# Layer 0 start-up of a fused attention and expert kernel: the first two batch rows are projected first, the other keys are projected dense and spread by transfers

## The reference

```python
x = x + xattn0(layernorm(x), ctx)     # 16 heads of 8; softmax(q k^T / sqrt(8)) v, out projection
x = x + ffn0(layernorm(x))            # 8 experts, each token goes to the one with the largest logit; relu^2
x = x + xattn1(layernorm(x), ctx)     # the same shape, scores clipped, other weights and biases
x = x + ffn1(layernorm(x))            # 8 experts, the best two by softmax(logits / 5), gelu
```

## Time and profile before

| | |
|---|---|
| median of 3 runs | 242.5 us (242.43 to 242.52) |
| profiled execution, first to last instruction | 242.5 us, so nothing of its time lies outside its span |
| PE busy | 225.4 us, 93% of the span |
| DVE, ACT, POOL busy | 164.2, 121.9, 79.8 us |
| mean granted clock of TensorE | 0.993 of full |
| start to first maxima of layer 0 | 16.84 us |

### The profile page before, as it was taken

How to read it: one execution, slowest core, us unless ns; L and a number is a source line. 1 busy time by engine, 2 the same in 40 slices (tenths; PEclk the granted TensorE clock), 3 DMA queues, 4 the chain that set the end, 5 groups by cost and what they waited for, 6 DMA issues and landing times.

```text
span 242.5 us, 6733 instructions
## 1 busy us (share of the span) xinstructions
PE 225.4 (93%) x2534; PEld 173.1 (71%) x2534; DVE 164.2 (68%) x513; ACT 121.9 (50%) x231; POOL 79.8 (33%) x105
## 2 busy tenths in 40 slices
PE   7999989999998999999987799998999999999993
PEld 7347668776666999998874556777656777766773
DVE  2697668656654865569438675797328974799994
ACT  2653456564674566655600377565435356443340
POOL 8592400001061177745450794564510100000000
PEclk9999999999999999999999999999979999999999
DMA  7990422314014013421122110213000000001001
GB/s 209 392 395 12 118 56 53 90 49 137 3 44 123 0 56 87 135 80 34 44 55 58 45 49 26 69 49 110 27 0 4 0 0 0 3 0 46 3 0 43
DMA packets 12451, 16.38 MB, mean 68 GB/s; under 512 B 1428, under 2 KB 9620, under 8 KB 12292
## 3 DMA queue, kind: packets, MB, share of 16 engines
q1 hardware_dynamic: 10068, 12.87, 17.2%
q0 software_dynamic: 1152, 2.24, 3.2%
q10 hardware_dynamic: 1200, 0.85, 1.1%
HBM read 11.31 MB, written 3.95 MB: 63 GB/s over the span
## 4 chain that ended last, share of the span: by engine, by line
PE 68%; DVE 17%; DMA 7%; issue 3%; POOL 2%; ACT 1%; DVEq 0%; ACTq 0%; SPq 0%; POOLq 0%
PE ps L1240 12%; PE ps L1252 12%; PE ps L1063 10%; PE ps L1108 6%; PE ps L1320 5%; PE ps L1330 5%; DVE mx L681 5%; PE ps L1071 4%; DVE xn L663 4%; PE ps L973 4%; DMA moe_y<-ys,tok_i 3%; DMA work<-moe_y 2%; DVE stats L649 2%; POOL rstd L367 2%; DMA xr<-in_x 2%
## 5 line engine op out<-in xcount | busy, mean ns | idle before, releaser
L681 DVE TENSOR_REDUCE mx<-ps 128x4 f32<-128x512 f32 x64 | 41.0, 685 | 15.6 <-PE ps L1063 15.6
L517 ACT ACTIVATE PT<-ps 128x512 f32<-128x512 f32 x64 | 35.7, 590 | 27.7 <-PE ps L1071 27.7
L1063 PE MATMUL ps<-k,q 32*128 32x128 f32 x512 | 36.1, 282 | 6.8 <-DVE mx L681 5.7
L1063 PEld LDWEIGHTS ps<-k,q 32*128 32x128 f32 x512 | 30.8, 186 | 16.2 <-DVE mx L681 12.9
L1071 PE MATMUL ps<-q,k 32*128 32x128 f32 x512 | 37.2, 283 | 0.0
L1252 PEld LDWEIGHTS ps<-proj,work 128*128 128x128 f32 x256 | 30.7, 192 | 5.7 <-issue 5.7
L627 ACT ACTIVATE work<-ps,fc 128x512 f32<-128x512 f32 x32 | 21.5, 687 | 24.4 <-PE ps L1240 22.9
L1071 PEld LDWEIGHTS ps<-q,k 32*128 32x128 f32 x512 | 31.1, 186 | 1.9 <-issue 1.7
L1240 PE MATMUL ps<-xT,fc 128*128 128x512 f32 x64 | 31.5, 617 | 0.0
L1252 PE MATMUL ps<-proj,work 128*128 128x128 f32 x256 | 31.1, 275 | 0.0
L403 POOL DMA_INDIRECT moe_y<-ys,tok_i x22 | 21.8, 991 | 24.1 <-DVE ys L899 12.0
(11 more groups left out here) (156 smaller groups left out, 314.4 us busy)
## 6 DMA issues: line engine op xcount, KB each, us to landing
proj<-in_proj SPq DMA_DIRECT2D x1, 2048.0 KB, 12.2
fc<-in_fc SPq DMA_DIRECT2D x8, 256.0 KB, 3.3
slots_x<-xs SPq DMA_DIRECT2D x2, 709.5 KB, 12.4
fc<-in_w SPq DMA_DIRECT2D x8, 129.0 KB, 2.3
proj<-in_w SPq DMA_DIRECT2D x8, 128.0 KB, 2.5
wr<-in_wr SPq DMA_DIRECT2D x1, 913.0 KB, 7.9
xs<-slots_x SPq DMA_DIRECT2D x2, 322.5 KB, 3.8
xs<-slots_x SPq DMA_DIRECT2D x2, 258.0 KB, 3.0
```

Source lines behind the costliest of these rows:

```text
L517: nc.scalar.activation(PT[:, j % PTR, :], ps[:, ring_at(layer, ("st", j)), :], ACT.Exp, scale=SCALE).then_inc(b_done, 1)
L681: nc.vector.tensor_reduce(mx[:, b, 4 * g:4 * g + 4], ps[:, S_BANK(layer, j), :].rearrange("p (k m) -> p k m", m=M), axis=AX, op=ALU.max).t ...
L1063: ins = mm(ps[:, S_BANK(layer, 2 * n + i), P * k:P * k + P], q4[r:r + 32, k, L * b:L * b + L], k4[r:r + 32, k, M * b:M * b + M], start=Tru ...
```

## The change

- Rows 0 and 1 are taken alone at first: statistics, `rsqrt`, normalisation (`first_normalise`), transposes, and queries and keys in products of 256 columns (`first_keys`, `queries(0, i)`). `ln_stats(0, 1)` then covers rows 2 to 7, whose normalisation stands in DVE steps 0, 1 and 2, two rows each.
- Keys of rows 2 and 3 (256 columns, step 0) and of rows 4 to 7 (512 columns, step 1) are each one dense product, spread by four SP transfers each (`keys_in`). Before them POOL writes the constants of `k4` (`k_fill`, two instructions that read zeros of `q4`, which ACT now clears).
- Queries of rows 2 and 3 follow in steps 2 and 3. The transposes of rows 4 to 7 and the values of rows 4 to 7 stand in step 4, the dense queries of rows 4 to 7 in step 5, the values of rows 0 to 3 in step 6. The idle products of layer 0 are gone.
- POOL clears `vaug` only after the last normalisation; `second_key_bias` stands in DVE step 3, `v_evac(1)` in step 4, `v_evac(0)` in step 6, `context_sums` in tile 5 of the expert layer.
- `proj` is loaded in eight pieces beside `fc`, the empty slots are written after rows 2 and 3, and `wa` is 128 + 1 columns wider (the dense key weights).

```diff
@@ SP
-            sp.dma_start(proj[:], proj_in).then_inc(s_fc, 16)
+            def keys_in(part, lo, hi):
+                for g in range(4):
+                    sp.dma_start(k4[32 * g:32 * g + DH, :, lo:hi],
+                                 k_dense[32 * g:32 * g + 32, lo - 256:hi - 256]).then_inc(k_in[part], 16)
@@ shift_rows
+                    if layer == 0 and b == 0:
+                        sp.wait_ge(k_sb, 6)
+                        keys_in(1, 512, 1024)
...
                         sp.dma_start(fc[:, b, :], fc_in[:, b, :]).then_inc(s_fc, 16)
+                        sp.dma_start(proj[:, b], proj_in[:, b]).then_inc(s_fc, 16)
+                    if layer == 0 and b in (2, 3):
+                        empty_slots(b - 2)
...
+            sp.wait_ge(k_fill, 1)
+            sp.wait_ge(k_sb, 5)
+            keys_in(0, 256, 512)
             shift_rows(0)
@@ POOL
             rsqrt(0, 0)
+            pool.wait_ge(first_norm, 1)
+            pool.wait_ge(dve_const, 1)
+            pool.wait_ge(q_fill, 1)
+            nc.gpsimd.tensor_scalar(k4[:, :, 256:512], q4[:, :, 512:768], shift_row[:, 0:1], None, ALU.subtract)
+            nc.gpsimd.tensor_scalar(k4[:, :, 512:1024], q4[:, :, 512:1024], shift_row[:, 0:1], None, ALU.subtract).then_inc(k_fill, 1)
             rsqrt(0, 1)
+            pool.wait_ge(ln_norm, 2)
             nc.gpsimd.memset(vaug[:], 0.0).then_inc(v_clear, 1)
...
-            nc.gpsimd.memset(q4[:, :, 512:1024], 0.0).then_inc(q_fill, 1)
+            pool.wait_ge(k_fill, 1)
+            pool.wait_ge(q_sb, Q_DONE[0])
+            for g in range(4):
+                pool.dma_start(q4[32 * g:32 * g + DH, :, 512:1024], q_dense[32 * g:32 * g + 32, 1, :]).then_inc(q_in[0], 16)
@@ ACT
+            nc.scalar.activation(q4[:, :, 512:1024], ones[:, 0:1].unsqueeze(2).to_broadcast([P, 4, N // 2]), ACT.Copy,
+                                 scale=0.0).then_inc(q_fill, 1)
...
+                    if layer == 0 and n == 0:
+                        dense_keys_evac(0, 256, 512)
+                    if layer == 0 and n == 1:
+                        more_ln_evac()
+                        dense_keys_evac(1, 512, 1024)
+                    if layer == 0 and n in (2, 3):
+                        queries_evac(1, 2 * n - 4)
+                        queries_evac(1, 2 * n - 3)
+                    if layer == 0 and n == 4:
                         ln_evac(0, 1)
+                    if layer == 0 and n == 5:
                         second_queries_evac()
@@ DVE
-                    if layer == 0 and n == 1:
-                        context_sums()
-                    if layer == 0 and n in (2, 3):
-                        v_evac(n - 2)
+                    if layer == 0 and n in (0, 1, 2):
+                        first_normalise(2 * n + 2, 2 * n + 4, (ln_norm, None, ln_norm)[n])
+                    if layer == 0 and n == 3:
+                        second_key_bias()
+                    if layer == 0 and n == 4:
+                        v_evac(1)
+                    if layer == 0 and n == 6:
+                        v_evac(0)
...
+                if t == 5:
+                    context_sums()
@@ PE second_half
                 if layer == 0 and n == 0:
+                    dense_keys(0, 256, 512)
+                if layer == 0 and n == 1:
+                    pe.wait_ge(ln_norm, 1)
+                    for i in range(2):
+                        ins = nc.tensor.transpose(ps[:, LN_BANK[0][0], 128 * i:128 * i + 128], xn[:, 2 + i, 0:D], ident[:])
+                    ins.then_inc(ln_tr, 1)
+                    pe.wait_ge(s_ctx[1], 16)
+                    dense_keys(1, 512, 1024)
+                if layer == 0 and n == 2:
                     pe.wait_ge(ln_xT, 1)
                     pe.wait_ge(k_sb, 5)
+                    queries(1, 0)
+                    queries(1, 1)
+                if layer == 0 and n == 3:
+                    pe.wait_ge(k_sb, 6)
+                    queries(1, 2)
+                    queries(1, 3)
+                if layer == 0 and n == 4:
+                    pe.wait_ge(q_sb, 8)
                     ln_transpose(0, 1)
+                    v_proj(0, 1)
+                if layer == 0 and n == 5:
+                    pe.wait_ge(ln_xT, 2)
+                    dense_queries(0)
+                if layer == 0 and n == 6:
+                    pe.wait_ge(q_sb, Q_DONE[0])
                     v_proj(0, 0)
@@ PE scores, scores_t
+                    if layer == 0 and n == 4:
+                        pe.wait_ge(k_in[0], 64)
+                        pe.wait_ge(q_sb, 8)
+                    if layer == 0 and n == 8:
+                        pe.wait_ge(k_in[1], 64)
+                        pe.wait_ge(q_in[0], 64)
...
-                    if m == 0 and layer == 0:
-                        pe.wait_ge(q_sb, 5)
+                    if m == 1 and layer == 0:
                         pe.wait_ge(v_sb, 1)
```

More of the change, by code:

```diff
@@ L365, in rsqrt @@
                 pool.wait_ge(ln_var, 2 * k + half + 1)
-                sl = slice(4 * half, 4 * half + 4)
+                sl = slice(4 * half, 4 * half + 4) if k else slice(6 * half and 2, 2 + 6 * half)
                 nc.gpsimd.tensor_tensor(rstd[:, sl], ve[:, sl], minus_half[:, sl], ALU.pow).then_inc(ln_rstd, 1)
@@ L645, in ln_stats @@
             def ln_stats(k, half):
-                bs = range(4 * half, 4 * half + 4)
-                sl = slice(4 * half, 4 * half + 4)
+                sl = slice(4 * half, 4 * half + 4) if k else slice(6 * half and 2, 2 + 6 * half)
+                bs = range(sl.start, sl.stop)
                 for b in bs:
@@ L665, in ln_normalise, with first_normalise @@
                 ins.then_inc(ln_norm, 1)
+            def first_normalise(lo, hi, done):
+                dve.wait_ge(ln_rstd, 1 if hi <= 2 else 2)
+                for b in range(lo, hi):
+                    ins = nc.vector.tensor_scalar(xn[:, b, 0:D], xr[:, b, :], mv[:, b, 0:1], rstd[:, b:b + 1],
+                                                  ALU.subtract, ALU.mult)
+                if done is not None:
+                    ins.then_inc(done, 1)
             def v_evac(half):
-                dve.wait_ge(v_ps, half + 1)
+                dve.wait_ge(v_ps, 2 - half)
                 dve.wait_ge(v_clear, 3)
@@ L1176, in attention @@
                         top_transpose(1)
[L1177 to L1178 removed]
+                    if layer == 1 and n in (4, 5):
                         idle_product(256)
```

205 lines of the change are left out of this document (106 added, 99 removed).

## The result

The changed kernel took 256.08 us (median of four, 253.8 to 256.72) beside 242.47 of the kernel before on the same chip: a ratio of 1.0542, interval 1.0503 to 1.058. The forecast was 243.1 with a range to 244.8, so it was wrong by 13 us, in the direction to which it gave the highest chance. The granted clock averaged 0.953 over the profiled execution.

A forecast was written before the change was run, and what follows sets the result against it. PE was taken as the bound (68% of the last chain). Start -4.4, steps 0 to 4 -1.45, step 4 to 5 +1.75, wait +4.05, traffic +0.4, expert layer +0.3: +0.65 on 242.5, predicted 243.1 us, range 240.8 to 244.8.

The forecast's parts named there:

- The step that failed: Start of layer 0: POOL's fill of `k4` takes 2.6 us, at most twice that, ending at 10.6 to 13.2.
- the second power: POOL's `rsqrt` for rows 2 to 7, after the fill: done 11.7 to 14.2, wanted by DVE at 13.7, taken as hidden.
- Rival B: The wait at step 8 also drops TensorE's clock, costing 1 to 1.5 us: 244.3 us; chance 0.12.
- rival A: Main forecast: PE waits 3.7 us at step 8 for query transfers, eating the start's gain; 242.1 to 244.0, chance 0.55.
- traffic: Before step 8: `fc`, `proj` and empty slots beside the query transfers delay their landing by 0.4 us, 1.5 at the end.
- Rival C: Query transfers before step 8 land faster, in 3.2 us: step 8 at 32.8 to 33.2, 241.5 us; chance 0.20.
- rival D: No wait at step 8 at all: step 8 at 30.7, 239.0 us; chance 0.13.
- First maxima: DVE's first maxima, step 0 of layer 0: begin at 12.4, 4.4 us earlier; right if 11.9 to 13.0.
- Step 4: Layer 0: starts at 20.5, 5.85 us earlier, with the transfers of the first keys and `mT` hidden.
- step 5: Layer 0: starts at 24.25, 4.1 us earlier; 1.75 of the gain goes into work between steps 4 and 5.
- The key bias: `second_key_bias` on DVE waits out POOL's clearing of `vaug` until 22.1; without that wait step 5 would be at 23.9.
- The expert layer: `context_sums` delays DVE's `xsT` copy of tile 7 and PE's transpose behind it: +0.3 us, bounds 0 and 0.6.

The follow-up runs named there:

- act_fill: Changed kernel with the `k4` constants written by ACT at the start instead of by POOL's fills: 246.73 us, ratio 1.0195.
- act_idle8: act_fill with twelve unread PE products of 256 columns ahead of step 8: 243.66 us, ratio 1.0068.
- idle_both: Changed kernel with unread PE products in both long waits, four in step 1 and twelve ahead of step 8: 247.6 us, ratio 1.0197.
- early_queries: act_fill with the dense queries' product and evacuation moved from step 5 to step 4: 241.31 us, ratio 0.9954.
- early_late_bias: early_queries plus three unread products ahead of step 8, with the second key bias in step 8 instead of step 3: 241.29 us, ratio 0.9957.
- early_one_proj: early_queries plus three unread products ahead of step 8, with `proj` loaded in one piece at the start: 240.53 us, ratio 0.9907.
- early_sp: early_queries with the four query transfers on SP's queue instead of POOL's: 244.69 us, ratio 1.0097.
- sp_queries: act_fill with the four query transfers on SP's queue instead of POOL's: 245.95 us, ratio 1.0167.

## Why the prediction was wrong

**The step that failed** is the one that read "POOL fills `k4` from 7.95: 3072 elements, 2.6 us at `vaug`'s 0.86 ns each, twice that if a read costs as much again", and "taken as hidden; at the far end it costs 0.5". Measured: 8.28 us, which is outside its own upper bound of 5.2. The bound was twice a row of another operation, when rows of the same operation stood in the page. The forecast had the second power done at 11.7, at the far end at 14.2. With 8.28 in its own chain that is 17.3 (7.95, 8.28 and 1.02); it was done at 17.6, and PE idles 3.15, six times the 0.5 of the far end. The fill was priced, its place was seen, and the size decided. The sum then had nothing for what such a gap does to the clock, and that was the larger part: 6.2 us against the stall's 3.3.

**Rival B was right in mechanism and in price, and it struck first at a place where I hadn't looked.** It had the clock fall behind the wait at step 8 and priced that at 1 to 1.5 us, with a chance of 0.12. It fell there and cost 1.5 (act_fill against act_idle8 at the end of layer 0's attention) or 1.2 (after against idle_both), so the price was right. It also fell in step 1 and cost 6.2. The forecast counted a fall after the wait among the signs that it was wrong. What spoke against it, the mean clock of 0.993 in a run that also has waits, was no argument: in before the longest wait of PE between 5 and 60 us is 0.6 us and the clock there is 1.00, and the change makes two gaps, of 3.15 and 5.26. The half speed in the price of B is the 0.50 of the earlier trace rows at 178 us; after's windows have 0.50 in both gaps, and with products in them the clock is 1.00 (idle_both). Why the fall in step 1 cost so much more stands in the rows: it lasted from 15.5 to 32.6 us, though PE is busy in all of 20 to 28, and the one of the second wait from 42.8 to 49.6, half of it in the wait.

**The wait at step 8 (rival A) held, and it was longer.** Forecast 3.7 us, 4.1 with traffic; measured 5.2 to 5.3. The evacuation ended at 27.60 in act_fill (forecast 27.3), and POOL's first issue came 0.74 later, as in the earlier trace rows. The term that was small is traffic: the last landing took 6.1 us, 1.7 over the earlier trace rows, where I took 0.4 and held 1.5 for the end. The block of empty slots in that term was taken as 355 KB; the page of after, as that of before, has it at 709.5 KB. early_queries, with the four issued ahead of these blocks and landed in 4.0 at most, fits with traffic as its cause; no run took the blocks away by themselves. Rival C, quicker landings, did not show in any run, and rival D, without a wait, neither. One small sum in these steps is off: by the terms given PE on its own is at step 8 at 30.55, not 30.7. It doesn't enter the forecast, since step 8 goes by the landing at 34.4.

**The start and steps 0 to 5 were right once the fill is out.** First maxima 13.02 in act_fill (forecast 12.4, and 11.9 to 13.0 counted as right) with the first key product at 6.33; 13.24 in after, with that product at 7.26, is just outside. Step 4 at 21.10 (20.5), step 5 at 24.65 (24.25). The key bias does sit out the clearing, 2.03 us; that it cost 0.35 is refuted by early_late_bias. The first keys, `mT` and `proj` in pieces were hidden, as said. The expert layer cost 0.2 for 0.3.

**What the change is worth** once both of its waits are mended: early_one_proj, 0.9% faster than before. The start's gain is real. It was lost to a fill that stood ahead of something needed, to a transfer started too late, and more than to either of them to the clock behind them: 7.4 of the 13.0 us, 6.2 of them behind the first.

## What to carry to other kernels

Before pricing a new instruction, look in the profile for its own operation on its own engine, however small the group, and make its rows the bounds; a row of another operation doubled is no bound. Where a change puts a gap of even a few us into TensorE's stream, price the clock behind it as well: here it cost more than the gaps did (7.4 us against 3.3 for the stall and 1.9 for the rest of the change). It fell in gaps of 2.80 (early_sp), 3.15 and 5.26 us (after) and not in one of 1.19 (early_queries), and a few products that nobody reads showed its cost in one run (idle_both). And where a transfer is late, try to start it earlier before moving it to another queue: here 1.78 us earlier brought step 8 forward by 3.8 (early_queries), while on SP's queue `mT` stood behind the queries and the weights and held step 8 in their place, by 4.90 (sp_queries).
